# A deformable convolution: high and low parts of a tap's transposed values by one instruction each over two PSUM banks, not one per bank

## The chip, the cores and the metric

The kernel runs on one NeuronCore of a Trainium2 chip. The metric is the device time of one execution in microseconds (us), the lower the better. PE is the matrix engine (TensorE), PEld its weight loads, ACT the scalar engine, DVE the vector engine, POOL the engine that issues the gathers, SP the one that issues most loads and stores.

## The reference, cut to what matters

The input `x` is 4 images of 1024 channels and 64x64 pixels. Layer 0 is a bottleneck with a deformable 3x3 convolution, layer 1 a masked, grouped bottleneck. The change lies in the deformable convolution:

```python
out = jax.nn.relu(frozen_bn(conv2d(x, w1, stride=1), g1, b1, m1, v1))        # 1024 -> 256 channels
offset = conv2d(out, w_off, pad=1, bias=b_off)                               # 18 offsets for each pixel
# deform_conv3x3: for each of the 9 taps four gathered corners, weighted and summed
val = gather(y0, x0) * (wy0 * wx0)[:, None] + gather(y0, x1) * (wy0 * wx1)[:, None] + ...
out = jnp.einsum('nckhw,ock->nohw', val, w.reshape(w.shape[0], w.shape[1], K))
out = jax.nn.relu(frozen_bn(out, g2, b2, m2, v2))
out = frozen_bn(conv2d(out, w3), g3, b3, m3, v3)                             # 256 -> 1024 channels
return jax.nn.relu(out + x)
```

Layer 1 multiplies by a mask, convolves in 4 groups (1x1, 3x3, 1x1), adds its input and clips at zero.

## The kernel before, in words

The work is cut into 32 blocks of 8 image rows (512 pixels). A software pipeline of 42 steps runs five stages on different blocks at once. Stage A (first convolution) works on block s, stage T (offsets) on s-1, stage B (deformable convolution) on s-8, stage C (third convolution and the first of layer 1) on s-9, and stage E (the rest of layer 1) on s-10. So stage B runs in steps 8 to 39, and steps 8 to 31 have stage A beside it. Each engine has its own queue with an order written by hand, and the engines meet by semaphores. Steps are written in pairs; the middle of the program is a loop over such pairs, and "even" and "odd" steps below are the two halves of a pair.

Stage B of one block goes through 9 taps. For each tap, POOL gathers four tiles of 128 pixels (each with its four corners) into 8 slots, so two taps' gathers are in flight. ACT multiplies the first corner (`corner0`, L698), DVE adds the other three (`interpolate`, L952, 12 instructions), and the sum lies in `val` with pixels in the partitions. PE turns it (`turn_val`, L482): 8 transposes of 128x128 into two PSUM banks `psV[0]` and `psV[1]`, one for each half m of the 256 channels. The product is made in split precision: ACT copies each bank, rounded, to `valT_hi` (`valT_copy`, L712), DVE subtracts that copy from the bank to get `valT_lo` (`valT_low`, L962). Then PE multiplies (`tap`, L501 to L503: 12 matmuls, three products for each m and each output half o).

`psV`, `valT_hi` and `valT_lo` exist once. So these waits tie the engines together:

- `turn_val(k)` needs `val` of tap k, and that DVE has read `psV` for tap k-1 (`valT_rest`).
- `valT_copy(k)` needs the turned values and that the matmuls of tap k-1 are through (`tap_done`).
- `valT_low(k)` needs `valT_copy(k)` (`valT_ready`).
- `tap(k)` needs both parts.

PE's order in one step is, for k from 0 to 8: the work of other stages that is listed beside tap k, then `turn_val(k)`, then `tap(k-1)`. While ACT and DVE split tap k, PE has the work that stands beside tap k+1:

```python
                    1: each(conv3, 2, 3),
                    2: [lambda: conv1(1, 0), lambda: conv1(1, 1)],
...
                    8: each(gconv3, 0) + [lambda: conv1(0, 0, ahead=1, chunks=[0])],
```

DVE's order puts `valT_low(k-1)` first in its list for tap k. The exceptions are tap 8, whose low part is made in the same step behind a part of the interpolation, and whatever stage work stands ahead of it. ACT's order for a tap is work of other stages, `valT_copy(k)`, `corner0(k+2)`; for tap 1 the work ahead of it is four `y_relu` (L731). The gather of tap k+2 is released when DVE has finished the interpolation of tap k.

## Time and profile before

| | |
|---|---|
| median of 3 runs | 3049.81 us (3049.41 to 3057.76) |
| the profiled execution | 3054.81 us, of it 3053.0 us between first and last instruction |
| PE busy | 2839.3 us, 93% |
| DVE busy | 2311.4 us, 76% |
| ACT busy | 1290.1 us, 42% |
| POOL busy | 1233.8 us, 40% |
| mean granted PE clock | 0.979 of full speed |

Busy times overlap, so they don't add up to the span. A row of the timeline gives the start, how long a run of like instructions took, the engine, the source line, the operation, output and inputs, and how many instructions were merged. A bracket at its end gives how long the engine had been idle before and what ended that idle time. A row with x2 whose time is 1.08 us is two instructions that overlap in part, not two of 0.54 us.

### The profile page before, as it was taken

The numbers are of one execution on the slowest core, as the hardware profiler recorded it, in microseconds if no ns is written. First come the engines' busy times: TensorE is split into PE (matmuls) and PEld (weight loads), VectorE is DVE, ScalarE is ACT, GpSimd is POOL, SyncE is SP. The second block draws the span as 40 slices with busy tenths as digits, with TensorE's granted clock in tenths as the row PEclk, the third lists the DMA queues.
The fourth block names the chain that finished last, engine by engine and source line by source line (L and its number), as shares of the span: only waits on it lengthen the run. The fifth ranks groups of instructions, "written<-read, shape, count | busy, mean of one in ns | idle before, by whom it ended". The sixth has DMA issues, their size and how long they took to land.

```text
span 3053.0 us, 45120 instructions
## 1 busy us (share of the span) xinstructions
PE 2839.3 (93%) x12064; PEld 1564.4 (51%) x12064; DVE 2311.4 (76%) x5439; ACT 1290.1 (42%) x2530; POOL 1233.8 (40%) x1160
## 2 busy tenths in 40 slices
PE   7978999999999999999999999999999999999998
PEld 3435555555555555555555545555555555555553
DVE  2238888887788878788877778888778888888871
ACT  1224444444444444444444444444444444444442
POOL 1035444433434443344443434444434455555540
PEclk9989999999999999999999999999999999999999
DMA  7768887888788888888788788888887788888872
GB/s 265 233 225 318 316 288 274 310 299 296 277 298 270 314 291 298 286 295 290 273 306 298 274 290 277 291 307 300 289 287 275 278 303 290 296 295 299 294 269 83
DMA packets 263070, 863.50 MB, mean 283 GB/s; under 512 B 31746, under 2 KB 72834, under 8 KB 254336
## 3 DMA queue, kind: packets, MB, share of 16 engines
q0 software_dynamic: 165888, 604.05, 57.1%
q1 hardware_dynamic: 78592, 190.68, 17.9%
q10 hardware_dynamic: 18432, 67.12, 5.4%
q8 instruction: 44, 0.72, 0.1%
q14 instruction: 114, 0.93, 0.1%
HBM read 747.72 MB, written 114.02 MB: 282 GB/s over the span
## 4 chain that ended last, share of the span: by engine, by line
PE 63%; DMA 13%; DVE 10%; issue 7%; POOL 3%; ACT 2%; DVEq 0%; SPq 0%; ACTq 0%; POOLq 0%
DMA corners<-corner_tables,samples_in 13%; PE psR L521 9%; PE psA L413 8%; PE psD L501 7%; PE psD L503 7%; PE psD L502 7%; PE psR L553 6%; PE psV L482 6%; DVE val L952 6%; PE psA L449 4%; PE psR L534 4%; PE psR L570 3%; POOL corners L378 3%; PE psD L449 1%; DVE y L935 1%
## 5 line engine op out<-in xcount | busy, mean ns | idle before, releaser
L378 POOL DMA_INDIRECT corners<-corner_tables,samples_in x1152 | 1221.7, 1061 | 1722.7 <-DVE val L952 1268.8
L952 DVE SCALAR_TENSOR_TENSOR val<-corners,samples_in,val 128x256 f32<-128x256 f32 x3456 | 1426.8, 477 | 220.0 <-ACT val L698 179.8
L698 ACT ACTIVATE val<-corners,samples_in 128x256 f32<-128x256 f32 x1152 | 517.5, 505 | 371.1 <-DMA corners<-corner_tables,samples_in 365.9
L712 ACT ACTIVATE valT_hi<-psV 128x512 fp32r<-128x512 f32 x576 | 311.7, 593 | 802.1 <-PE psD L503 655.0
L521 PE MATMUL psR<-deformed,w_sb 128*128 128x512 f32 x1024 | 490.3, 620 | 60.3 <-DVE y L883 51.0
L962 DVE TENSOR_TENSOR valT_lo<-psV,valT_hi 128x512 fp32r<-128x512 f32 x576 | 370.0, 684 | 217.1 <-ACT valT_hi L712 216.6
L501 PE MATMUL psD<-valT_hi,w_hi 128*128 128x512 f32 x1152 | 488.8, 424 | 0.4 <-DVE valT_lo L962 0.4
L502 PE MATMUL psD<-valT_hi,w_lo 128*128 128x512 f32 x1152 | 460.1, 399 | 0.0
L503 PE MATMUL psD<-valT_lo,w_hi 128*128 128x512 f32 x1152 | 460.1, 399 | 0.0
L482 PEld LDWEIGHTS psV<-const_sb,val 128*128 128x128 f32 x2304 | 266.3, 143 | 240.9 <-issue 134.2
L482 PE MATMUL psV<-const_sb,val 128*128 128x128 f32 x2304 | 313.5, 279 | 72.9 <-DVE valT_lo L962 65.9
L413 PE MATMUL psA<-x_sb,w_sb 128*128 128x512 f32 x768 | 357.2, 604 | 6.2 <-DMA x_sb<-in_x 6.0
L521 PEld LDWEIGHTS psR<-deformed,w_sb 128*128 128x128 f32 x1024 | 195.2, 198 | 292.9 <-issue 197.1
L731 ACT ACTIVATE y<-y,bn_shift 128x512 f32<-128x512 f32 x256 | 179.7, 720 | 253.1 <-DVE y L883 253.0
L553 PE MATMUL psR<-ga,gw_sb 64*64 64x512 f32 x2304 | 261.5, 594 | 2.7 <-DVE ga L912 1.9
L501 PEld LDWEIGHTS psD<-valT_hi,w_hi 128*128 128x128 f32 x1152 | 220.9, 192 | 60.7 <-issue 17.8
L503 PEld LDWEIGHTS psD<-valT_lo,w_hi 128*128 128x128 f32 x1152 | 219.3, 190 | 54.0
L502 PEld LDWEIGHTS psD<-valT_hi,w_lo 128*128 128x128 f32 x1152 | 221.0, 192 | 42.3 <-issue 1.9
L413 PEld LDWEIGHTS psA<-x_sb,w_sb 128*128 128x128 f32 x768 | 140.7, 190 | 190.0 <-issue 177.6
L883 DVE SCALAR_TENSOR_TENSOR y<-psR,bn_scale,y 128x512 f32<-128x512 f32 x256 | 189.4, 742 | 28.5 <-PE psR L521 28.5
L570 PE MATMUL psR<-gb,gw_sb 64*128 64x512 f32 x512 | 144.5, 641 | 31.7 <-DVE gb L927 14.4
L553 PEld LDWEIGHTS psR<-ga,gw_sb 64*64 64x64 f32 x2304 | 83.0, 132 | 150.2 <-issue 150.2
(78 smaller groups left out, 1566.3 us busy)
## 6 DMA issues: line engine op xcount, KB each, us to landing
y<-in_x SPq DMA_DIRECT2D x128, 512.0 KB, 7.4
out<-y ACTq DMA_DIRECT2D x128, 512.0 KB, 7.7
x_sb<-in_x SPq DMA_DIRECT2D x48, 1024.0 KB, 8.3
corner_tables<-x_sb SPq DMA_DIRECT2D x128, 256.0 KB, 5.4
corners<-corner_tables,samples_in POOLq DMA_INDIRECT x1152, 6.0
y<-in_x SPq DMA_DIRECT2D x8, 2048.0 KB, 10.2
corner_tables<-corners SPq DMA_DIRECT2D x8, 1139.0 KB, 5.7
samples_dram<-samples SPq DMA_DIRECT2D x32, 90.0 KB
```

What stands on the lines that cost most here:

```text
L378: nc.gpsimd.indirect_dma_start(corners[:, slot, :], None, table, bass.IndirectOffsetOnAxis(ap=index[:, TAPS * t + k:TAPS * t + k + 1], axi ...
L413: mm = pe.matmul(psA[m][:], w1_sb[:, half * KC // 2 + k, m * P:(m + 1) * P], y[:, bpar, half * KC // 2 + k, :] if blow < LAG_B else x_sb[: ...
L482: mm = pe.transpose(psV[m][:, tile * P:(tile + 1) * P], val[:, (par + k) % 2, tile, m * P:(m + 1) * P], ident)
L501: pe.matmul(psD[o][:], w2_hi[:, m, k, chunk], valT_hi[:, m, :], start=first, stop=False)
L502: pe.matmul(psD[o][:], w2_lo[:, m, k, chunk], valT_hi[:, m, :], start=False, stop=False)
L503: mm = pe.matmul(psD[o][:], w2_hi[:, m, k, chunk], valT_lo[:, m, :], start=False, stop=last)
L521: mm = pe.matmul(psR[m % 2][:], w3_sb[:, k, m * P:(m + 1) * P], deformed[:, k, :], start=k == 0, stop=k == MC - 1)
L553: mm = pe.matmul(psR[half][64 * slot:64 * slot + 64, :], gw2_sb[rows, slot, j, :], ga[rows, par, slot, ky:ky + ROWS, kx:kx + IMG], start=j ...
L698: nc.scalar.activation(val[:, (bpar + k) % 2, tile, :], corners[:, n % GS, 0:CMID], ACT.Copy, scale=samples_in[:, bpar, w:w + 1]).then_inc ...
L712: nc.scalar.activation(valT_hi[:, m, :], psV[m][:], ACT.Copy).then_inc(valT_ready, 1)
L952: nc.vector.scalar_tensor_tensor(acc, corners[:, n % GS, corner * CMID:(corner + 1) * CMID], samples_in[:, bpar, w:w + 1], acc, ALU.mult, ...
L962: nc.vector.tensor_tensor(valT_lo[:, m, :], psV[m][:], valT_hi[:, m, :].bitcast(F32), ALU.subtract).then_inc(valT_rest, 1)
```

## The change

The two banks of `psV` become one PSUM tensor of 1024 values for each partition, `psV_both`; the names `psV[0]` and `psV[1]` are kept as its halves. ACT's two copies become one of 1024 values and DVE's two subtractions one of 1024. The semaphores `val_turned`, `valT_ready` and `valT_rest` count once for each tap, where they counted twice. The transposes go tile by tile with m inside, where they went m by m. `turn_val` waits once for `valT_rest` before its first transpose, where it waited before each half. `tap` waits once, before its first matmul, and for `valT_rest` alone.

```diff
-        psV = [ctx.enter_context(nc.psum_tensor(f"psV{i}", [P, 512], F32)) for i in range(2)]
+        psV_both = ctx.enter_context(nc.psum_tensor("psV", [P, MC * PIX], F32))
+        psV = [psV_both[:, i * PIX:(i + 1) * PIX] for i in range(MC)]
...
-                    for m in range(MC):
-                        if low > LAG_B or k >= 1:
-                            pe.wait_ge(valT_rest, 2 * (TAPS * h + k - 1) + m + 1)
-                        for tile in range(TILES):
+                    if low > LAG_B or k >= 1:
+                        pe.wait_ge(valT_rest, TAPS * h + k)
+                    for tile in range(TILES):
+                        for m in range(MC):
                             mm = pe.transpose(psV[m][:, tile * P:(tile + 1) * P],
                                               val[:, (par + k) % 2, tile, m * P:(m + 1) * P], ident)
-                        mm.then_inc(val_turned, 1)
+                    mm.then_inc(val_turned, 1)
...
                     for m in range(MC):
-                        pe.wait_ge(valT_ready, 2 * (TAPS * h + k) + m + 1)
-                        pe.wait_ge(valT_rest, 2 * (TAPS * h + k) + m + 1)
+                        if m == 0:
+                            pe.wait_ge(valT_rest, TAPS * h + k + 1)
...
-                        act.wait_ge(val_turned, 2 * (TAPS * block + k - 1))
+                        act.wait_ge(val_turned, TAPS * block + k - 1)
...
-                    for m in range(MC):
-                        act.wait_ge(val_turned, 2 * (TAPS * h + k) + m + 1)
-                        nc.scalar.activation(valT_hi[:, m, :], psV[m][:], ACT.Copy
-                                             ).then_inc(valT_ready, 1)
+                    act.wait_ge(val_turned, TAPS * h + k + 1)
+                    nc.scalar.activation(valT_hi[:].rearrange("p m x -> p (m x)"), psV_both[:], ACT.Copy
+                                         ).then_inc(valT_ready, 1)
...
-                    for m in range(MC):
-                        dve.wait_ge(valT_ready, 2 * (TAPS * h + k) + m + 1)
-                        nc.vector.tensor_tensor(valT_lo[:, m, :], psV[m][:],
-                                                valT_hi[:, m, :].bitcast(F32), ALU.subtract
-                                                ).then_inc(valT_rest, 1)
+                    dve.wait_ge(valT_ready, TAPS * h + k + 1)
+                    by_pair = lambda a: a.rearrange("p m x -> p (m x)")
+                    nc.vector.tensor_tensor(by_pair(valT_lo[:]), psV_both[:], by_pair(valT_hi[:]).bitcast(F32),
+                                            ALU.subtract).then_inc(valT_rest, 1)
```

On PE, in the loop over the middle steps, the turn of tap 2 stands behind the 8 matmuls of the first convolution (L413, in the changed kernel L414) that cover the split of tap 1. Before:

```order
L413 MATMUL psA<-x_sb,w_sb 128x512 [waits x_in]
L413 MATMUL psA<-x_sb,w_sb 128x512 x3
L474 REGISTER_ALU
L480 ISA [waits fma]
L482 MATMUL psV<-const_sb,val 128x128 [waits valT_rest]
L482 MATMUL psV<-const_sb,val 128x128 x3
L480 REGISTER_ALU
L482 MATMUL psV<-const_sb,val 128x128 [waits valT_rest]
L482 MATMUL psV<-const_sb,val 128x128 x3
L501 MATMUL psD<-valT_hi,w_hi 128x512 [waits valT_rest,valT_ready]
```

and in the changed kernel:

```order
L414 MATMUL psA<-x_sb,w_sb 128x512 [waits x_in]
L414 MATMUL psA<-x_sb,w_sb 128x512 x3
L475 REGISTER_ALU
L480 REGISTER_ALU [waits fma]
L483 MATMUL psV<-const_sb,val 128x128 [waits valT_rest]
L483 MATMUL psV<-const_sb,val 128x128 x7
L502 MATMUL psD<-valT_hi,w_hi 128x512 [waits valT_rest]
```

The order of the work is the same. The second wait, between the fourth and the fifth transpose, is gone, and the first one now stands for the whole low part of the tap before.

On ACT, at the same place of the program, the split of tap 1 stands behind the four `y_relu` (L731) and ahead of the first corners of tap 3 (L698, in the changed kernel L699). Before:

```order
L731 ACTIVATE y<-y,bn_shift 128x512 [waits y_sum] x4
L707 ISA
L711 REGISTER_ALU [waits tap_done]
L712 ACTIVATE valT_hi<-psV 128x512 [waits val_turned]
L711 REGISTER_ALU
L712 ACTIVATE valT_hi<-psV 128x512 [waits val_turned]
L693 ISA
L696 REGISTER_ALU [waits val_turned]
L698 ACTIVATE val<-corners,samples_in 128x256 [waits gathered0]
```

and in the changed kernel:

```order
L731 ACTIVATE y<-y,bn_shift 128x512 [waits y_sum] x4
L708 ISA
L711 REGISTER_ALU [waits tap_done]
L712 ACTIVATE valT_hi<-psV 128x1024 [waits val_turned]
L697 REGISTER_ALU [waits val_turned]
L699 ACTIVATE val<-corners,samples_in 128x256 [waits gathered0]
```

Nothing moved past anything else; two copies became one, and a register instruction or two went with them. DVE's order changes in the same way, two L962 of 128x512 to one of 128x1024.

## Rows read from the trace of the kernel before

**Rows 1.** The page: the span, and the chain that ended last, by engine.

```profile
span 3053.0 us, 45120 instructions
...
PE 63%; DMA 13%; DVE 10%; issue 7%; POOL 3%; ACT 2%; DVEq 0%; SPq 0%; ACTq 0%; POOLq 0%
```

**Rows 2.** The page's costliest groups: count, busy us, mean ns, idle before them.

```profile
L698 ACT ACTIVATE val<-corners,samples_in 128x256 f32<-128x256 f32 x1152 | 517.5, 505 | 371.1 <-DMA corners<-corner_tables,samples_in 365.9
L712 ACT ACTIVATE valT_hi<-psV 128x512 fp32r<-128x512 f32 x576 | 311.7, 593 | 802.1 <-PE psD L503 655.0
...
L962 DVE TENSOR_TENSOR valT_lo<-psV,valT_hi 128x512 fp32r<-128x512 f32 x576 | 370.0, 684 | 217.1 <-ACT valT_hi L712 216.6
...
L731 ACT ACTIVATE y<-y,bn_shift 128x512 f32<-128x512 f32 x256 | 179.7, 720 | 253.1 <-DVE y L883 253.0
```

**Rows 3.** Groups of instructions by shape, whole run: a DVE subtraction of 1024 columns.

```profile
L1011 DVE TENSOR_TENSOR w_lo<-x_sb,w_hi 128x1024 fp32r<-128x1024 f32 x1 | 1.2, 1217 | 0.0
```

**Rows 4.** Timeline of all engines about the turn of tap 8, step 21.

```profile
1421.60 1.08 ACT L712 ACTIVATE valT_hi<-psV 128x512 fp32r<-128x512 f32 x2 [5.08 <-PE psD L503]
1422.23 1.29 DVE L962 TENSOR_TENSOR valT_lo<-psV,valT_hi 128x512 fp32r<-128x512 f32 x2 [0.52 <-ACT valT_hi L712]
...
1422.48 1.13 PE L413 MATMUL psA<-x_sb,w_sb 128*128 128x512 f32 x2
1422.57 1.70 ACT L698 ACTIVATE val<-corners,samples_in 128x256 f32<-128x256 f32 x4
...
1423.44 1.28 DVE L935 TENSOR_TENSOR y<-psR,y 128x512 f32<-128x512 f32 x2
1423.44 1.04 PE L482 MATMUL psV<-const_sb,val 128*128 128x128 f32 x8
```

**Rows 5.** The chain that ended last, about the turn of tap 2, step 21.

```profile
1372.37 0.59 ACT valT_hi L712
...
1372.98 0.70 DVE valT_lo L962
...
1373.72 1.25 PE psV L482 x8
1374.97 0.24 PE psD L501
```

**Rows 6.** Timeline of all engines about the turn of tap 1, step 23.

```profile
1541.62 1.28 DVE L962 TENSOR_TENSOR valT_lo<-psV,valT_hi 128x512 fp32r<-128x512 f32 x2
...
1542.36 0.93 PE L482 MATMUL psV<-const_sb,val 128*128 128x128 f32 x5 [0.20 <-DVE valT_lo L962]
```

**Rows 7.** PE's timeline: the turn of tap 2, and the next transposes, in five steps.

```profile
1011.98 1.25 PE L482 MATMUL psV<-const_sb,val 128*128 128x128 f32 x8 [2.36 <-DVE valT_lo L962]
...
1015.88 1.04 PE L432 MATMUL psA<-const_sb,mid 128*128 128x128 f32 x8
...
1193.61 1.25 PE L482 MATMUL psV<-const_sb,val 128*128 128x128 f32 x8 [3.29 <-DVE valT_lo L962]
...
1556.83 1.71 PE L482 MATMUL psV<-const_sb,val 128*128 128x128 f32 x8 [2.73 <-DVE valT_lo L962]
...
2193.40 1.94 PE L482 MATMUL psV<-const_sb,val 128*128 128x128 f32 x8 [3.45 <-DVE valT_lo L962]
...
2199.71 1.03 PE L432 MATMUL psA<-const_sb,mid 128*128 128x128 f32 x8
...
2285.34 1.94 PE L482 MATMUL psV<-const_sb,val 128*128 128x128 f32 x8 [3.93 <-DVE valT_lo L962]
```

**Rows 8.** Windows: busy us by engine, then PE's granted clock, DMA share, GB/s.

```profile
1012.00:1018.00 6.00, 6.00 (x31) 4.54 (x32) 6.00 (x15) 4.46 (x11) 2.60 (x3) 1.00 0.86 293
...
2193.40:2199.40 6.00, 6.00 (x19) 5.09 (x20) 5.25 (x13) 2.54 (x6) 2.60 (x3) 0.53 0.84 285
```

**Rows 9.** Windows about the start of an odd step, columns as in rows 8.

```profile
1525.00:1530.00 5.00, 4.68 (x18) 1.92 (x16) 3.82 (x10) 3.02 (x7) 0.00 (x0) 1.00 0.26 107
...
1540.00:1545.00 5.00, 4.62 (x19) 2.86 (x20) 3.69 (x9) 0.51 (x1) 3.07 (x3) 1.00 1.04 432
```

**Rows 10.** Timeline of all engines about a turn in step 35, without stage A.

```profile
2649.49 1.28 DVE L962 TENSOR_TENSOR valT_lo<-psV,valT_hi 128x512 fp32r<-128x512 f32 x2
...
2650.69 1.27 DVE L952 SCALAR_TENSOR_TENSOR val<-corners,samples_in,val 128x256 f32<-128x256 f32 x3
...
2650.93 0.82 PE L482 MATMUL psV<-const_sb,val 128*128 128x128 f32 x6
```

## The prediction, made before the changed kernel had run

> **What bounds the kernel now.** I read the page first. PE has 63% of the chain that ended last, the gathers' DMA 13% and DVE 10% [rows 1]. So time is lost or won where PE waits, and at the start of a step, where the gathers end last. The groups come next [rows 2]: DVE stood idle 216.6 us before the low part of a tap, each time released by ACT's high part, while ACT itself was idle 655.0 us waiting for PE's last matmul. Neither engine is short of time there. What counts is latency: from the moment PE frees `valT_hi` until PE may overwrite `psV`. The third view is the timeline about each turn of a tap, to see how much other work covers that latency.
>
> At the turn of tap 8 the cover is thin [rows 4]. ACT starts at 1421.60, DVE at 1422.23, and PE, busy until then with two half-matmuls of the first convolution, turns at 1423.44 without any idle time. At the turn of tap 2 in odd steps there is no cover left [rows 5]: the chain runs ACT, DVE, PE. ACT's copies stand late there, behind four `y_relu` that wait for the values gathered at the step's start.
>
> **The duration of the new pair.** A DVE subtraction of 1024 columns took 1.217 us from SBUF [rows 3]; I take it for PSUM too: it is 0.53 us more than the 0.684 of the low part's 512 columns [rows 2], about a column a nanosecond. No row has an ACT copy of 1024 columns. From below: ACT took 505 ns for 256 columns and 593 for 512 [rows 2], other operand kinds, and by that slope 1024 take 0.77 us. From above: two copies took 1.08 us end to end [rows 4]. Between them, 505 ns for 256 columns and 720 for 512 with a bias [rows 2] give 0.84 ns a column, hence 0.593 + 0.430 = 1.02 us, which I take because both rows have per-partition operands and the slope is the steeper, surer one.
>
> What the engines save is small. The pair holds ACT 0.97 us (1421.60 to 1422.57) and DVE 1.21 us (1422.23 to 1423.44) [rows 4]. One instruction of 1.02 or 1.217 us, overlapping its successor by some 0.08 as these do, holds them 0.94 and 1.14. That is 0.03 and 0.07 us for each of 288 taps, 29 us of engine time in all, costed at nothing: at most taps both wait for PE's matmuls, and that idle time swallows it. If this cover were gone it would be worth those 29 us.
>
> **What the pair's latency does.** Before, DVE began 0.61 us after ACT (1372.37 to 1372.98), PE began to turn 0.74 after that, at 1373.72, needing only the first half, and was through at 1374.97 [rows 5], 2.60 us after ACT's start. The turn took 1.25 and not the usual 1.04 [rows 4], because its second half waited for DVE too. Now the steps are ACT 1.02, hand-over 0.04, DVE 1.217, hand-over 0.06: PE may start 2.34 us after ACT and is through 1.04 later, at 3.38. So a turn that waits loses 3.38 - 2.60 = 0.78 us. Where DVE comes late of its own and ACT has long finished, before was 0.74 + 1.25 = 1.99 after DVE's start [rows 5, 6], now 1.217 + 0.06 + 1.04 = 2.32: a loss of 0.33.
>
> I went through all 288 taps with this arithmetic, taking for each the starts of ACT, DVE and PE from the timeline. Four terms remain.
>
> 1. *Turn of tap 8, steps 8 to 31.* ACT starts at 1421.60, so PE may start at 1423.94, and it was ready at 1423.44: 0.50 us lost [rows 4]. All 24 steps show a loss, 0.32 to 0.75; together **12.0 us**. Nothing behind it absorbs the shift: the last taps, the output adds, the last interpolation and the next gathers all follow PE.
> 2. *Turn of tap 2, odd steps from 11 to 29 and steps 12, 30 and 31*: 13 places, with a wait for `valT_rest` of 1.94 to 3.93 us (five shown) [rows 7]. Nine run at full clock and lose 0.78 each, 7.0 us. Four run at the low clock, where the second half didn't wait separately, and lose the whole later start, 2.34 - 1.35 = 0.99 each, 4.0 us. Together **11.0 us**.
> 3. *The clock.* In the same places PE's wait grows. The row at 1011.98, after 2.36 us of idle time, and the one at 1193.61, after 3.29, ran at clock 1.00, which is 2.4 GHz. Those at 2193.40 and 2285.34, after 3.45 and 3.93, ran near 0.53, the level of 1.2 GHz for most of the window, and the one at 1556.83 after 2.73 did too in part, with another short wait just before [rows 7, 8]. From turn to the next transposes 3.90 us passed at full clock (1011.98 to 1015.88) and 6.31 at the low one (2193.40 to 2199.71) [rows 7]. The 3.90 holds 0.21 us of waiting for the second half, so a fall costs 2.6 us, and 1.6 where it is partial (two of the four such places). I take 2.1. The wait grows by 0.99, less 0.33 because the turn of tap 1 and with it the first convolution start later [rows 6], so by 0.66. Nine waits of 1.94 to 3.29 become 2.6 to 3.95; six of them become longer than the 3.45 of the row at 2193.40. Six at 2.1 are **12.6 us**, with 0 and nine at 2.6, 23 us, as the ends.
> 4. *Steps 8 to 10*, where PE still waits at other taps: about **2 us**, an estimate by the same two prices.
>
> The turn of tap 1 in odd steps starts late by 0.33 [rows 6], but the turn of tap 2 then waits for DVE anyway, so this costs nothing. In even steps it has room. In the last eight steps, without stage A, DVE frees `psV` 1.28 us after its start, at 2650.77, where PE turned at 2650.93 [rows 10]: 0.16 us of cover, so nothing is lost. The matmuls' single wait costs nothing at taps 0 to 7, as the next turn has already waited for the same event; at tap 8 six more matmuls stand between, which cover it.
>
> The sum is 12.0 + 11.0 + 12.6 + 2 = 37.6 us. On the profiled execution that is 3054.8 + 37.6 = 3092. That execution lies 5 us above the median of 3049.81, so against the median I expect 3087.
>
> A rule of the skill speaks against this change. The Trainium skill, Perfetto Trace Analysis, section Optimizing Scalar/DVE Operations, says that where Scalar and Vector aren't saturated but cause bubbles on other engines, breaking up instructions may let work complete sooner. The change does the reverse, and the rows agree with the rule: ACT and DVE idle, PE waits.
>
> The same section advises grouping into larger operations if the engine is saturated; by that the 29 us of engine time would be a gain, which is the rival on the other side below.
>
> **The rivals.**
>
> - *Waits alone, no new falls of the clock.* Terms 1, 2 and 4: 25 us, 3075. For it: the row at 1193.61 kept the full clock after 3.29 us of idle time. Against it: the one at 1556.83 did not after 2.73 [rows 7]. The Trainium skill, TensorE: Matmul & The Clock Gate, section HAM oscillation, tells of waits between groups of matmuls that throw the clock to half; by that page more of the nine would fall.
> - *All nine fall, and ACT's copy takes 1.08.* Term 3 is 23 us, terms 1 and 2 grow by 0.06 x 37 = 2: 50 us, 3100. Each further 0.1 us of the pair, should two banks cost extra, adds 0.1 x 37 = 3.7 us.
> - *Hidden anyway.* The 12 odd steps start with gathers at a DMA share of 1.04, so a later PE might cost nothing there. But at 1525 to 1530, when the shift arrives, the share is 0.26 [rows 9], so the queue isn't backlogged. If hidden, half of term 1 goes. With ACT at 0.77 the waits shrink by 0.25 x 37 = 9 more. Both and no clock fall: 25 - 6 - 9 = 10 us, 3060, the edge of no change.
> - *Faster: engine time counts after all.* If ACT's and DVE's own occupancy set the pace, 29 us are gained, 3021. It decides only where neither waits for PE between two taps; the idle sums of [rows 2] are against it.
>
> **How the numbers follow.** Forecast with four to nine falls 0.48, waits alone 0.26, above that 0.06, hidden to within 0.3% (9 us, about what a measurement of this kernel can tell from no change) 0.14, faster 0.06. The range 3062 to 3102 takes in the first two and part of the third. Slower 0.80, same 0.14, faster 0.06.
>
> **What the profile after would show.** ACT's L712 at about 1.02 us and DVE's L962 at 1.217. DVE's idle time before the low part up by about 0.4 us at each tap where it waited. PE's idle time before the transposes, for `valT_lo`, up by some 20 us, with waits of about 0.5 at tap 8, where there were none. The turn of tap 2 in odd steps after waits above 3 us, more of them at the low clock. Wrong would be: transposes of tap 8 without a wait (then ACT's copy is much shorter than 1.02), or a step's start that absorbs the shift.

## The result: slower by 2.0%, more than was predicted

| | median | lowest to highest | runs |
|---|---|---|---|
| before, beside it | 3053.78 us | 3049.41 to 3058.21 | 4 |
| changed | 3116.68 us | 3108.91 to 3118.46 | 4 |

The ratio is 1.0203, with an interval from 1.0181 to 1.0225: 63 us more. Predicted were 3087 us and a range up to 3102, so the sign was right and the size too small. The profiled execution of the changed kernel took 3108.91 us, at the lower end of its runs, and its mean granted clock was 0.971 against 0.979.

The page of the changed kernel, with the rows that answer to [rows 1, 2] and the gathers' group. A group's row has count, busy us, mean ns, then the idle time before it. The gathers' group of the kernel before stands first, as it was not among the rows shown:

```profile
L378 POOL DMA_INDIRECT corners<-corner_tables,samples_in x1152 | 1221.7, 1061 | 1722.7 <-DVE val L952 1268.8
```

and the changed kernel:

```profile
span 3107.1 us, 43186 instructions
...
PE 62%; DVE 12%; DMA 10%; issue 9%; ACT 3%; POOL 2%; DVEq 1%; SPq 0%; ACTq 0%; POOLq 0%
...
L379 POOL DMA_INDIRECT corners<-corner_tables,samples_in x1152 | 1246.1, 1082 | 1750.2 <-DVE val L952 1297.2
...
L712 ACT ACTIVATE valT_hi<-psV 128x1024 fp32r<-128x1024 f32 x288 | 293.7, 1020 | 838.2 <-PE psD L504 649.6
L962 DVE TENSOR_TENSOR valT_lo<-psV,valT_hi 128x1024 fp32r<-128x1024 f32 x288 | 352.1, 1223 | 304.0 <-ACT valT_hi L712 264.5
```

The two durations are those that were worked out: 1.020 us for ACT and 1.223 for DVE. So there is no surprise in the instructions themselves. DVE's idle time behind ACT grew from 216.6 to 264.5 us. One row moved that the prediction never looked at: the gathers on POOL take 1246.1 us for the same 1152 instructions, 24 us more than their 1221.7 before. The sum alone doesn't tell the time, though: after_pad16 below has 1246.9 us there too and is 34 us faster.

**The turn of tap 8 (answers to [rows 4]).** Timeline of the changed kernel, step 21.

```profile
1440.33 1.02 ACT L712 ACTIVATE valT_hi<-psV 128x1024 fp32r<-128x1024 f32 x1 [4.77 <-PE psD L504]
...
1441.20 1.12 PE L414 MATMUL psA<-x_sb,w_sb 128*128 128x512 f32 x2
...
1441.38 1.23 DVE L962 TENSOR_TENSOR valT_lo<-psV,valT_hi 128x1024 fp32r<-128x1024 f32 x1 [0.58 <-issue]
...
1442.66 1.09 PE L483 MATMUL psV<-const_sb,val 128*128 128x128 f32 x8 [0.34 <-DVE valT_lo L962]
```

PE turns 2.33 us after ACT's start, where 2.34 was worked out. The turn now stands behind 0.34 us of idle time. From L414's start to the turn pass 1.46 us, before it was 0.96 from L413's start: the 0.50 us of term 1. Over the whole trace PE's idle time before the transposes grew from 72.9 to 93.8 us, the "some 20 us" that was forecast.

**The turn of tap 2 (answers to [rows 7, 8]).** PE's timeline of the changed kernel in three of the thirteen steps, from the turn to the next transposes.

```profile
840.97 1.09 PE L483 MATMUL psV<-const_sb,val 128*128 128x128 f32 x8 [2.86 <-DVE valT_lo L962]
844.70 1.04 PE L433 MATMUL psA<-const_sb,mid 128*128 128x128 f32 x8
...
1206.60 1.10 PE L483 MATMUL psV<-const_sb,val 128*128 128x128 f32 x8 [3.19 <-DVE valT_lo L962]
1211.88 0.38 PE L433 MATMUL psA<-const_sb,mid 128*128 128x128 f32 x2
...
1574.81 1.09 PE L483 MATMUL psV<-const_sb,val 128*128 128x128 f32 x8 [2.12 <-issue]
```

The windows of the first two, where the third figure from the right is PE's granted clock:

```profile
840.97:844.70 3.73, 3.73 (x21) 3.14 (x21) 3.73 (x10) 1.61 (x3) 1.15 (x1) 1.00 0.93 293
...
1206.60:1211.88 5.28, 5.28 (x20) 4.29 (x21) 4.69 (x12) 1.61 (x3) 2.11 (x2) 0.68 0.77 287
```

The piece takes 3.73 us at the full clock and 5.28 where the clock had fallen after 3.19 us of idle time: a fall costs 1.55 us. In step 19 it is new; before, 3.29 us of idle time there left the clock at 1.00 [rows 7]. In step 23 the wait even became shorter, 2.12 after 2.73 us. The row of step 19 ends with the view's window, so its x2 is not the whole group.

The turn of tap 1 in step 23, which answers to [rows 6]:

```profile
1560.65 1.21 DVE L962 TENSOR_TENSOR valT_lo<-psV,valT_hi 128x1024 fp32r<-128x1024 f32 x1
...
1561.92 1.09 PE L483 MATMUL psV<-const_sb,val 128*128 128x128 f32 x8 [0.73 <-DVE valT_lo L962]
```

PE turns 1.27 us after DVE's start, where it had turned after 0.74, and takes 1.09 us instead of 1.25 (in [rows 6] 0.93 of it are shown, as the row is cut at the window's edge): through at 2.36, worked out 2.32.

**The steps without stage A (answers to [rows 10]).** Here lies what the prediction missed. First PE's timeline in step 35 of the kernel before, behind the turn of tap 6 at 2642.55. L570 is a grouped convolution of stage E, L576 adds the input by a matmul, and behind them comes the turn of tap 7 at 2650.93 [rows 10].

```profile
2648.05 1.13 PE L570 MATMUL psR<-gb,gw_sb 64*128 64x512 f32 x4 [1.60 <-DVE gb L927]
2649.10 1.98 PE L576 MATMUL psR<-y,const_sb 128*128 128x512 f32 x4
```

The same place of the changed kernel, from turn to turn:

```profile
2674.11 1.09 PE L483 MATMUL psV<-const_sb,val 128*128 128x128 f32 x8
...
2681.60 1.21 PE L571 MATMUL psR<-gb,gw_sb 64*128 64x512 f32 x4 [3.59 <-DVE gb L927]
2682.74 3.55 PE L577 MATMUL psR<-y,const_sb 128*128 128x512 f32 x4
2686.13 1.04 PE L483 MATMUL psV<-const_sb,val 128*128 128x128 f32 x8
```

and the windows of its two halves:

```profile
2677.80:2681.60 3.80, 0.21 (x1) 0.00 (x1) 3.32 (x8) 2.13 (x4) 0.69 (x1) 1.00 0.99 362
2682.74:2686.13 3.39, 3.39 (x7) 1.40 (x5) 3.39 (x7) 1.50 (x3) 2.76 (x3) 0.53 0.50 118
```

From turn to turn 8.38 us became 12.02. PE waits 3.59 us for DVE's `gb` instead of 1.60, and behind the longer wait it runs at clock 0.53, near the level of 1.2 GHz, so that four matmuls take 3.55 us instead of 1.98. Why `gb` is late is seen on POOL and DVE, some 10 us earlier. The kernel before:

```profile
2633.49 1.19 POOL L378 DMA_INDIRECT corners<-corner_tables,samples_in  x1 [5.64 <-DVE val L952]
...
2633.78 1.28 DVE L962 TENSOR_TENSOR valT_lo<-psV,valT_hi 128x512 fp32r<-128x512 f32 x2
...
2634.98 0.94 POOL L378 DMA_INDIRECT corners<-corner_tables,samples_in  x1 [0.30 <-issue]
...
2634.98 4.84 DVE L952 SCALAR_TENSOR_TENSOR val<-corners,samples_in,val 128x256 f32<-128x256 f32 x12
...
2636.22 1.24 POOL L378 DMA_INDIRECT corners<-corner_tables,samples_in  x1 [0.30 <-issue]
...
2637.77 2.87 POOL L378 DMA_INDIRECT corners<-corner_tables,samples_in  x1 [0.30 <-issue]
```

and the changed kernel:

```profile
2665.05 1.19 POOL L379 DMA_INDIRECT corners<-corner_tables,samples_in  x1 [5.63 <-DVE val L952]
...
2665.35 1.22 DVE L962 TENSOR_TENSOR valT_lo<-psV,valT_hi 128x1024 fp32r<-128x1024 f32 x1
...
2666.48 4.83 DVE L952 SCALAR_TENSOR_TENSOR val<-corners,samples_in,val 128x256 f32<-128x256 f32 x12
...
2666.55 1.22 POOL L379 DMA_INDIRECT corners<-corner_tables,samples_in  x1 [0.30 <-issue]
...
2668.08 4.05 POOL L379 DMA_INDIRECT corners<-corner_tables,samples_in  x1 [0.30 <-issue]
...
2672.43 0.94 POOL L379 DMA_INDIRECT corners<-corner_tables,samples_in  x1 [0.30 <-issue]
...
2675.96 0.49 DVE L952 SCALAR_TENSOR_TENSOR val<-corners,samples_in,val 128x256 f32<-128x256 f32 x1 [2.18 <-ACT val L699]
2678.28 2.07 DVE L952 SCALAR_TENSOR_TENSOR val<-corners,samples_in,val 128x256 f32<-128x256 f32 x5 [1.83 <-ACT val L699]
2680.26 1.28 DVE L927 SCALAR_TENSOR_TENSOR gb<-psR,maskx 128x512 f32<-128x512 f32 x2
```

Read POOL against DVE. In both kernels the gathers of a tap, but for the first, fall beside or just behind twelve interpolations that DVE runs with nothing between them (called a stretch below). One gather is much longer than the others, and is called held here. It ends 0.82 us after the last of the twelve: before, 2637.77 + 2.87 = 2640.64 and 2634.98 + 4.84 = 2639.82; changed, 2668.08 + 4.05 = 2672.13 and 2666.48 + 4.83 = 2671.31. What differs is which gather it is. Before, it is the fourth, that begins 2.79 us into the stretch. In the changed kernel DVE passes from the low part to the stretch sooner (2665.35 to 2666.48 are 1.13 us, where 2633.78 to 2634.98 are 1.20), so the stretch begins before the second gather instead of with it. That gather takes 1.22 us instead of 0.94, and the third is caught 1.60 us into the stretch and held for 4.05. The fourth then can begin only at 2672.43, 1.12 us after the stretch's end; before, it had ended 0.82 us after that point. Its corners come late, the first corner on ACT too, DVE waits 2.18 and 1.83 us (before 0.38 and 2.02) ahead of `gb`, and PE waits for `gb`.

In most of the steps from 32 on, two taps' gathers meet such a stretch. There are 14 held gathers of 4.04 to 4.06 us instead of 13 of 2.86 to 2.87. Fourteen times 1.18 us are 16.5 us.

### The profile page after: what moved, and what is told of

Same layout as the page of the kernel before. It is cut to its first block, busy times and chain, and to the rows that moved or that the text cites. A ratio compares the mean times of both kernels' runs of the same rounds, so it can differ in the third digit from the quotient of the medians.

```text
span 3107.1 us, 43186 instructions
## 1 busy us (share of the span) xinstructions
PE 2856.0 (92%) x12064; PEld 1570.8 (51%) x12064; DVE 2290.9 (74%) x5151; ACT 1274.7 (41%) x2242; POOL 1258.1 (40%) x1160
## 4 chain that ended last, share of the span: by engine, by line
PE 62%; DVE 12%; DMA 10%; issue 9%; ACT 3%; POOL 2%; DVEq 1%; SPq 0%; ACTq 0%; POOLq 0%
DMA corners<-corner_tables,samples_in 10%; PE psR L522 9%; PE psA L414 7%; PE psD L502 7%; PE psD L503 7%; PE psD L504 7%; DVE val L952 6%; PE psV L483 6%; PE psR L554 6%; PE psA L450 4%; PE psR L535 4%; PE psR L571 2%; DVE valT_lo L962 2%; POOL corners L379 2%; PE psR L577 1%
## 5 line engine op out<-in xcount | busy, mean ns | idle before, releaser
L379 POOL DMA_INDIRECT corners<-corner_tables,samples_in x1152 | 1246.1, 1082 | 1750.2 <-DVE val L952 1297.2
L699 ACT ACTIVATE val<-corners,samples_in 128x256 f32<-128x256 f32 x1152 | 515.8, 500 | 370.1 <-DMA corners<-corner_tables,samples_in 352.8
L712 ACT ACTIVATE valT_hi<-psV 128x1024 fp32r<-128x1024 f32 x288 | 293.7, 1020 | 838.2 <-PE psD L504 649.6
L962 DVE TENSOR_TENSOR valT_lo<-psV,valT_hi 128x1024 fp32r<-128x1024 f32 x288 | 352.1, 1223 | 304.0 <-ACT valT_hi L712 264.5
L483 PE MATMUL psV<-const_sb,val 128*128 128x128 f32 x2304 | 311.0, 279 | 93.8 <-DVE valT_lo L962 76.5
L414 PE MATMUL psA<-x_sb,w_sb 128*128 128x512 f32 x768 | 356.5, 603 | 5.2 <-DMA x_sb<-in_x 5.2
L731 ACT ACTIVATE y<-y,bn_shift 128x512 f32<-128x512 f32 x256 | 179.3, 718 | 272.2 <-DVE y L883 247.7
L414 PEld LDWEIGHTS psA<-x_sb,w_sb 128*128 128x128 f32 x768 | 141.2, 190 | 187.2 <-issue 177.3
```

The source lines that it names most:

```text
L379: nc.gpsimd.indirect_dma_start(corners[:, slot, :], None, table, bass.IndirectOffsetOnAxis(ap=index[:, TAPS * t + k:TAPS * t + k + 1], axi ...
L414: mm = pe.matmul(psA[m][:], w1_sb[:, half * KC // 2 + k, m * P:(m + 1) * P], y[:, bpar, half * KC // 2 + k, :] if blow < LAG_B else x_sb[: ...
L483: mm = pe.transpose(psV[m][:, tile * P:(tile + 1) * P], val[:, (par + k) % 2, tile, m * P:(m + 1) * P], ident)
L699: nc.scalar.activation(val[:, (bpar + k) % 2, tile, :], corners[:, n % GS, 0:CMID], ACT.Copy, scale=samples_in[:, bpar, w:w + 1]).then_inc ...
L712: nc.scalar.activation(valT_hi[:].rearrange("p m x -> p (m x)"), psV_both[:], ACT.Copy).then_inc(valT_ready, 1)
L962: nc.vector.tensor_tensor(by_pair(valT_lo[:]), psV_both[:], by_pair(valT_hi[:]).bitcast(F32), ALU.subtract).then_inc(valT_rest, 1)
```

## Where the time went

The stretches between PE's turns, added up in each trace, give the table. Single executions differ by several us in parts whose code is the same. The changed kernel, after_pad16, after_pad384 and after_break have the changed code in the steps with stage A; the kernel before, without_a, before_pad384 and before_break have the old code there. So the rows for steps 8 to 31 compare the means of four traces with four.

| part | predicted | measured | from |
|---|---|---|---|
| turn of tap 7 to turn of tap 8, steps 11 to 31 | 10.5 of 12.0 | 10.8 | 133.3 - 122.5 |
| the rest of steps 11 to 31 (terms 2 and 3) | 23.6 | 10.7 | 1924.2 - 1902.7, less 10.8 |
| steps 8 to 10 | 2, and 1.5 of term 1 | 8.0 | 251.75 - 243.75 |
| steps 32 to 39 | 0 | 35.8 | 647.3 - 611.5, this kernel's trace |

The sum is 65 us, and the medians differ by 63. The first row is firm: its four traces lie at 132.2 to 134.1 us, the four of before at 122.4 to 122.7. The second is less so, since the four traces of before differ by 12 us among themselves over steps 11 to 31. By place, those 10.7 us are 3.8 between the turns of taps 0 and 1, 2.4 between 1 and 2, 4.2 between 2 and 3, and 0.4 behind the turn of tap 8. In the last row 30.1 us lie between the turns of taps 6 and 7 of the seven steps 33 to 39. Of these, 16.4 are PE's idle time before the first matmul on `gb` (26.6 us in all instead of 10.2), and 13.7 are what passes from there to the turn (35.2 instead of 21.4, each rounded): all seven ran at the low clock, before only one had.

## The experiments

All are built on the kernel before or on the changed one. Each median stands beside the kernel before on the same chip: 3051.51 us for the first four, 3056.83 for the next four, 3054.81 for the last four. The ratio is not exactly the quotient of the two medians; it differs from it by up to 0.0016.

| kernel | what it has | median us | ratio (interval) |
|---|---|---|---|
| with_a | one instruction each in steps with stage A | 3095.22 | 1.0135 (1.0106 to 1.0164) |
| without_a | one instruction each in the other steps | 3081.41 | 1.0107 (1.0076 to 1.0138) |
| dve_one | two high parts, one low part | 3131.00 | 1.0256 (1.0226 to 1.0285) |
| act_one | one high part, two low parts | 3073.08 | 1.0066 (1.0040 to 1.0092) |
| after_pad16 | changed, 0.07 us of DVE work behind a low part | 3082.51 | 1.0088 (1.0066 to 1.0110) |
| after_pad384 | changed, 0.38 us of it | 3071.00 | 1.0062 (1.0041 to 1.0083) |
| before_pad384 | before, 0.38 us of it | 3048.13 | 0.9974 (0.9960 to 0.9989) |
| after_break | changed, DVE's long stretches broken up | 3080.73 | 1.0076 (1.0054 to 1.0099) |
| split_7 | with_a, tap 7 with two instructions | 3074.49 | 1.0061 (1.0043 to 1.0079) |
| split_1 | with_a, tap 1 with two instructions | 3073.82 | 1.0063 (1.0045 to 1.0081) |
| split_017 | with_a, taps 0, 1 and 7 with two | 3057.63 | 1.0007 (0.9992 to 1.0023) |
| before_break | before, DVE's long stretches broken up | 3045.49 | 0.9967 (0.9954 to 0.9981) |

### Which steps, and which engine

The kernel keeps both forms and chooses by the step (`on` lists the stages of a step) or by the engine. `tap` keeps its two pairs of waits everywhere in these kernels and in the split ones below, where the changed kernel has one wait.

```diff
+        psV_both = ctx.enter_context(nc.psum_tensor("psV", [P, MC * PIX], F32))
+        one_copy = lambda on: "A" in on       # without_a: "A" not in on; act_one: True; dve_one: False
+        one_low = lambda on: "A" in on        # without_a: "A" not in on; act_one: False; dve_one: True
+        one_turn = lambda on: "A" in on       # without_a: "A" not in on; act_one, dve_one: False
...
+                    if one_copy(on):
+                        act.wait_ge(val_turned, 2 * (TAPS * h + k) + 2)
+                        nc.scalar.activation(by_pair(valT_hi[:]), psV_both[:], ACT.Copy).then_inc(valT_ready, 2)
+                        return
```

Steps with stage A alone:

> One instruction for each part in the steps that have stage A beside B (8 to 31), two as before in steps 32 to 39. Theory 1 (two places, two causes: PE waits longer at the turns of taps 8 and 2 in the middle steps, and something separate in the last eight): about half of the loss, +20 to +28 us over the kernel before (3054), so 3074 to 3082, and the turn of tap 7 in steps 33 to 39 as before. Rival (one cause, a state of the transfers that the middle steps hand on to the last ones): the whole +62.

Steps without stage A alone:

> The reverse: one instruction for each part in steps 32 to 39 alone. Theory 1: +28 to +34 us, so 3082 to 3088, all of it between the turns of taps 6 and 8 and at the step's end in steps 33 to 39, with gathers on POOL that take 4.05 us where 2.86 stood. Rival: no loss, since the middle steps are those of before.

The steps with stage A cost 44 us, where 20 to 28 were expected, and those without it 30, as expected. The second number is the clear one: where the prediction had put nothing lies nearly half of the loss. The trace of without_a has 30.1 us between the turns of taps 6 and 7, as the changed kernel has, and the same 14 gathers held for 4.04 to 4.06 us. Together the two are 74 us, 11 more than the whole change. The three intervals together leave some 15 us either way, so this doesn't show that the two halves interact. The trace of with_a, its fastest execution of five, shows some 37 of its 44 (34 in steps 8 to 31, against the mean of four, and 2.5 behind them). A part of that is the experiment's own: its turn of tap 8 waits 0.46 us in most steps, where the changed kernel has 0.34, which over the 21 steps from 11 on is 2.6 us.

Two high parts and one low part:

> Two high parts as before, one low part of 1024 columns, in all steps. Theory 1 with the gathers' hold set by where DVE's low part ends (0.07 us sooner with one instruction): the tail's +31 us remains, the middle is about the same as in the changed kernel, since the low part starts after 1.08 us of copies, not 1.02: about +60, 3114. Rival (the longer copy on ACT is what hurts): most of the loss gone, below +20.

One high part and two low parts:

> One high part of 1024 columns, two low parts and the two waits of the turn as before. Theory 1: the tail as before, with holds of 2.86 us. In the middle PE may start a turn 0.45 us later than before where DVE waits for ACT: 0.45 x 13 = 6 us at tap 2, 0.17 x 24 = 4 at tap 8, so +10, 3064. Rival (ACT's copy hurts): +40 or more.

The groups of the high and low part, first in dve_one, then in act_one:

```profile
L730 ACT ACTIVATE valT_hi<-psV 128x512 fp32r<-128x512 f32 x576 | 311.6, 592 | 832.5 <-PE psD L517 680.4
L980 DVE TENSOR_TENSOR valT_lo<-psV,valT_hi 128x1024 fp32r<-128x1024 f32 x288 | 352.0, 1222 | 327.8 <-ACT valT_hi L730 327.5
```

```profile
L726 ACT ACTIVATE valT_hi<-psV 128x1024 fp32r<-128x1024 f32 x288 | 294.1, 1021 | 833.6 <-PE psD L517 656.6
L985 DVE TENSOR_TENSOR valT_lo<-psV,valT_hi 128x512 fp32r<-128x512 f32 x576 | 370.2, 684 | 269.4 <-ACT valT_hi L726 268.8
```

The one low part is the costly half of the change. It costs 80 us alone, where 60 were expected, and more than the change itself. It must wait for two copies that take longer than one (1.08 against 1.02 us), and DVE's idle time behind ACT is 327.5 us. But 0.06 us at the 37 places where PE waits are an estimate of 2 us, so most of the excess over the change is not explained. The one high part alone costs 22, which makes 3073 where 3064 was expected. As dve_one keeps the old order of the transposes and both waits of the turn and of `tap`, and loses more, neither the new order nor the single waits are needed for the loss; they weren't run alone. The tail tells the two apart as well: dve_one has 14 gathers of 4.05 us and 31.8 us more between the turns of taps 6 and 7, act_one has 13 of 2.87 us and 1.9 more. So the long holds come with DVE's single subtraction, whatever ACT does.

### Is it the moment at which the gathers meet DVE's stretch?

If 0.07 us less between gather and stretch cause the hold, giving DVE 0.07 us back should undo it. In the steps without stage A a write to an unused tile stands behind the low part of taps 0 to 7; it takes 0.07 us with 16 columns and 0.38 with 384. Nothing of the computation changes.

```diff
+        pad_sb = sb("pad_sb", [P, 16])        # pad384: [P, 384]
...
+                    nc.vector.memset(pad_sb[:], 0.0).then_inc(padded, 1)
...
+                if "A" not in on:
+                    for k in range(1, TAPS):
+                        beside[k].insert(1, lambda k=k: pad(k))
```

> The changed kernel with one small write more on DVE (16 columns, to a tile nobody reads) behind each low part in steps 32 to 39 but for tap 8's, so that the interpolation there starts later by some 0.05 to 0.1 us, about where two low parts would have let it start. Theory 2 (the tail's loss is gathers on POOL that are held until a stretch of twelve interpolations ends, and which gather is held is decided by where its start falls in that stretch): the holds go back from 4.05 to 2.86 us or vanish, and the time falls by 25 to 32 us from 3117 although DVE has more to do. Rival (the low part's own later end costs the tail its time, by latency): the same 3117 or up to 3 us more.

> The same with 384 columns, which moves the stretch by some 0.3 to 0.5 us. Theory 2: the gathers start at other places of the stretch, near those of the middle steps, which were not held (their fourth gather began 2.38 us into the stretch, the held ones 2.78): no holds of 2.86 or 4.05 in the tail, time 25 to 50 us below 3117. Rival: 8 steps x 8 x 0.4 us more work on DVE, +0 to +15 over 3117.

> The kernel before (two instructions for each part) with the same write of 384 columns behind each low part in steps 32 to 39. Theory 2: the 13 holds of 2.86 us in the tail vanish or change; without them each saves about 1.9 us of a gather, so 3054 falls by up to 20 us. Rival: equal or slower by up to 10 us.

POOL and DVE in step 35 of after_pad16:

```profile
2662.10 0.07 DVE L976 MEMSET pad_sb<- 128x16 f32 x1
...
2662.13 0.94 POOL L382 DMA_INDIRECT corners<-corner_tables,samples_in  x1 [0.30 <-issue]
...
2663.38 1.22 POOL L382 DMA_INDIRECT corners<-corner_tables,samples_in  x1 [0.31 <-issue]
...
2664.90 2.86 POOL L382 DMA_INDIRECT corners<-corner_tables,samples_in  x1 [0.30 <-issue]
```

The pattern of the kernel before is back: 0.94, 1.22, and 2.86 us for the fourth gather. A program with 64 writes more is 34 us faster than the changed kernel (3116.68 to 3082.51; each has its own runs of the kernel before beside it, and the two ratios are 1.0203 and 1.0088). The stretch between the turns of taps 6 and 7 falls to 5.4 us above the kernel before, where it had been 30.1.

With 384 columns no gather of the tail is held at all, in either kernel: the fourth begins 2.27 us into the stretch there, takes 0.94, and both traces have 6 us less than the kernel before between the turns of taps 6 and 7. The write's own time is paid at the turn of tap 2 (1 to 2: about 10 us), but before_pad384 is still faster than the kernel before by 0.26%.

### Or is it the stretch itself?

Moving the gathers' moment and breaking DVE's stretch are two ways to the same end. Here the same 16-column write stands between the first and second four of the twelve interpolations, and between the second and third four, at the two places of a step where all twelve run without a break.

```diff
+                if "A" not in on:
+                    for n, (k, i) in enumerate([(5, 3), (5, 2), (7, 3), (7, 2)]):
+                        beside[k].insert(i, lambda n={(5, 2): 0, (5, 3): 1, (7, 2): 2, (7, 3): 3}[k, i]: pad(n + 1))
```

> The changed kernel with the small write of 16 columns between the three corners of two interpolations in steps 32 to 39 (those made in the lists of taps 5 and 7), so that the start of the stretch stays where it was and the stretch is broken in three. Theory 2 with the hold lasting until DVE's row of like instructions is interrupted: a hold ends at the first break behind its start, at most 1.7 us, and the time falls by 20 to 30 us from 3117. If such a break doesn't free POOL, the holds last 4.1 to 4.2 us and the time stays at 3117.

> The kernel before, with the small write of 16 columns between the three corners of two interpolations in steps 32 to 39 (four for each step). Theory of the held gathers: the holds of 2.86 us in the tail go, as in the changed kernel with the same breaks, and the time falls by 5 to 12 us below the kernel before (3046 for 3055), as with the write of 384 columns. Rival (it was the later start alone that helped): 3055.

POOL and DVE in step 35 of after_break, where the gathers begin as in the changed kernel:

```profile
2664.87 2.07 DVE L955 SCALAR_TENSOR_TENSOR val<-corners,samples_in,val 128x256 f32<-128x256 f32 x5
2664.93 1.22 POOL L382 DMA_INDIRECT corners<-corner_tables,samples_in  x1 [0.30 <-issue]
2666.46 0.94 POOL L382 DMA_INDIRECT corners<-corner_tables,samples_in  x1 [0.30 <-issue]
2666.49 0.07 DVE L976 MEMSET pad_sb<- 128x16 f32 x1
2667.70 1.23 POOL L382 DMA_INDIRECT corners<-corner_tables,samples_in  x1 [0.30 <-issue]
```

and in step 35 of before_break:

```profile
2628.76 0.07 DVE L977 MEMSET pad_sb<- 128x16 f32 x1
2629.93 0.94 POOL L381 DMA_INDIRECT corners<-corner_tables,samples_in  x1 [0.30 <-issue]
...
2639.26 1.13 PE L573 MATMUL psR<-gb,gw_sb 64*128 64x512 f32 x4 [0.65 <-DVE gb L930]
```

In after_break the third gather, which began 1.60 us into the stretch and took 4.05 us in the changed kernel, begins 1.59 us behind the stretch's start (2664.87 to 2666.46) and takes 0.94. The view merges the fifth interpolation, which starts beside the write, with the four before it, hence x5. No gather of the tail is held in either kernel, and in before_break PE's idle time before the matmul on `gb` is 0.65 us in step 35, where 1.60 was. The changed kernel comes down to 3080.73 us. The kernel before becomes faster than it was by 0.33% (0.19 to 0.46), 3045.49 against 3054.81: 32 writes that compute nothing save 9 us. It beats both kernels and has the lowest ratio of all, though before_pad384's interval overlaps with its.

### What is left in the steps with stage A

With the tail as before, with_a is split again at single taps. Splitting tap 7 gives PE back its early turn of tap 8, splitting tap 1 that of tap 2. The code below is cut to the choice of the taps.

```diff
+        SPLIT = (7,)                          # split_1: (1,); split_017: (0, 1, 7)
+        one = lambda on, k: "A" in on and k % TAPS not in SPLIT
```

> One instruction for each part in the steps with stage A but for tap 7, which is split by two instructions each, as everything in steps 32 to 39. Compared with the run of one instruction in all taps of those steps (3095, its turns of tap 8 13.4 us late in sum). Theory: the turn of tap 8 waits no longer, 12 to 14 us less, 3082. Rival (the loss there is taken back by a wait further on, since the next step's start waits for the gathers anyway): 3093 or more.

> The same with tap 1 alone split in two. Theory: the turn of tap 2 in odd steps starts 0.99 us and ends 0.78 us sooner, 11 us, and up to 13 more if fewer of these places run at the low clock: 3071 to 3086. Rival (what the turn of tap 2 loses is nothing, as the profiled run showed 0.9 us there): 3093 or more.

> Taps 0, 1 and 7 split in two, the others by one instruction, in the steps with stage A. Theory: every turn that had no cover is as before, and the six merged taps have cover, so the time is that of the kernel before, 3054 to 3062, with some 14 us less busy time on DVE and ACT that nobody needs. Rival (merged taps cost or give something by themselves): more than 10 us away from it.

By medians with_a is 43.7 us above the kernel before, split_7 19.7, split_1 19.0, and split_017 2.8, which can't be told from nothing. So all of the loss in these steps lies at taps 0, 1 and 7, and the six other taps may have their single instructions at no cost that can be measured: PE has other work there, as the prediction said. Splitting tap 7 and splitting tap 1 give 24 and 25 us, each with some 10 us of doubt either way by the intervals. For split_7 that is more than the 12 to 14 us expected, but not clear of them, and the 49 us together are more than the 41 that all three taps give. Tap 0 wasn't split alone. The traces show the two waits that were meant. In split_7 the turn of tap 8 has no idle time before it in steps 10 to 30, where with_a has 0.46 to 0.74 us. In split_1 the thirteen waits before the turn of tap 2 sum to 31.2 us, where with_a has 43.8 and the kernel before 38.9. (The profiled execution of split_7, 3089.3 us, is the longest of its six, so its sums are not used.)

## Why the prediction was wrong

In short: the steps with stage A were forecast to lose 37.6 us and lost about 30, and the last eight steps were forecast to lose nothing and lost 36. The sign was right for a reason, since the first part of the loss is there and is where it was said to be. That the two errors point different ways, and so leave the total at 63 and not at 73 or more, is luck.

**Right.** Both durations, to 0.01 us (1.020 for 1.02, 1.223 for 1.217). PE may turn 2.33 us after ACT's start for the 2.34 worked out. Term 1: 0.50 us at the turn of tap 8 in each middle step, 10.8 us of the 10.5 that it had there. The taps with other work beside them cost nothing, as split_017 shows.

**Mis-sized: terms 2 and 3, the turn of tap 2 and the clock, 23.6 us for a measured 10.7.** Term 3 had nine places at the full clock before, and six new falls at 2.1 us. The trace of before has seven of the thirteen at the low clock already, not four; one that was counted as full is step 13:

```profile
647.81 1.25 PE L482 MATMUL psV<-const_sb,val 128*128 128x128 f32 x8 [3.23 <-DVE valT_lo L962]
...
653.26 1.03 PE L432 MATMUL psA<-const_sb,mid 128*128 128x128 f32 x8
```

From turn to transposes 5.45 us passed there, against 3.90 at the full clock, the same 1.55 that a fall costs in the changed kernel. In the means of four traces 5.5 places become 9.75, and 4.25 falls at 1.55 are 6.6 us where 12.6 stood, which leaves some 4 us for term 2, where 11.0 stood. The thirteen waits grew from 36.4 to 42.1 us, 0.45 us each and not the 0.66 of term 3; and from the turn to the next transposes 0.17 us less pass at the full clock (3.73 for 3.90), which takes 2.2 us back. Against that, 3.8 us were lost between the turns of taps 0 and 1, where the prediction had put nothing. The four and four traces leave each of these sums some us of doubt. The rival "waits alone" came nearer in size, with 11.0 for both, though its ground was wrong: the clock did fall more often. The step that failed is "nine run at full clock", and with it "six of them become longer than the 3.45": a bound on the length of the wait told neither where the clock fell before nor where it fell afterwards.

**Mis-sized: steps 8 to 10**, 8.0 us where 2 and their part of term 1 (1.5) stood. The trace of the changed kernel has, over the three steps together, 1.0 to 1.3 us more in each of the stretches between the turns of taps 0, 1, 2 and 3, 2.8 more from tap 5 to tap 6, and 1.6 behind tap 8. This was not taken apart further.

**The step that failed, and made the forecast too small: "In the last eight steps, without stage A [...] 0.16 us of cover, so nothing is lost."** The 0.16 us was right for PE and `psV`, and it was the wrong question. Nothing is lost at the turn; the loss came by way of POOL. That engine stands in none of the prediction's sums. The chain is: DVE's pair is 0.07 us shorter; the third gather begins 1.60 us into a stretch of twelve interpolations instead of 1.24; it is held for 4.05 us; the corners behind it are late; `gb` is late by 2 us; PE's wait passes 3 us and the clock falls to 0.53. The experiments show the first links, and that the loss between these turns hangs on them; the links from the corners to PE's clock are read from the traces. after_pad16 breaks the chain at its first link, after_break at its second, and each takes the 30 us away: between those turns 5.4 us more than the kernel before are left in the one, 4.1 less than it in the other.

**Failed with it: the engine time "costed at nothing".** The 0.07 us for each tap were looked at as a gain that might be hidden or not, 29 us at most. They were a loss: a shorter instruction moved the gathers to a worse moment against DVE. The rival "faster" looked at the right quantity with the wrong sign; that its 29 us are near the 30 that were lost there is chance, since the loss isn't made of these 0.07 us.

The rule in the Trainium skill, Perfetto Trace Analysis, section Optimizing Scalar/DVE Operations, that breaking up instructions may help where Scalar and Vector aren't saturated but cause bubbles elsewhere, is borne out in the middle steps: splitting tap 1 and tap 7 again is worth 24 to 25 us each by the medians, with the doubt given above.

**What stays open.** Where a gather is held is known in part, and the cause is not known. Counted over all fourteen traces, for stretches of twelve with no other row between: of the gathers that began 1.58 to 1.60 us into one, 49 of 57 were held; at 2.77 to 2.79, 103 of 105; at 2.38 to 2.40, all in the steps with stage A, 25 of 110; about 1.24 and at 2.26 to 2.27, none. So the position goes with the hold but doesn't settle it. Some gathers are held for 1.7 to 3.3 us in steps 11 to 31, 5 of them before and 4 changed. One kind of these, a pair of 2.5 and 1.9 us behind the turn of tap 1, can be priced: in the even steps from 12 to 28 of the seven kernels that have it, the 30 steps with the pair took 92.9 us in the mean and the 33 without it 92.3. A kernel that has both the broken stretches and single instructions at taps 2 to 6 and 8 wasn't run; by split_017 and before_break I estimate that it would be no faster than before_break, since those single instructions gave nothing.

## What to carry to other kernels

Merging two instructions into one saves engine time and adds latency; look first for the waits that the first half used to release, and price only those places. Then ask what a few hundredths of a microsecond do to everything else that the engine works beside: here gathers issued by POOL were held by an unbroken run of vector instructions, and a shift of 0.07 us between the two cost 30 us. Where a POOL row with a steady duration shows an odd long one, lay it beside DVE's timeline, and try a tiny instruction of another kind in the middle of the run.

## What the runs showed of the hardware

**A gather instruction on POOL is held by an unbroken stretch on DVE.** In the last eight steps the held ones ended 0.82 us after the last of twelve SCALAR_TENSOR_TENSOR of 128x256 (4.83 us), after 2.87 or 4.05 us instead of 0.94 to 1.24. A MEMSET of 16 columns (0.07 us) between two of the twelve let them through. All ten kernels with the unbroken stretch at or near its usual place (after_pad16 among them) had 10 to 14 such holds in the last eight steps; the four with a shifted or broken one (after_pad384, before_pad384, after_break, before_break) had none.

The Trainium skill, SBUF — State Buffer, section Who interferes with whom, says that DVE and GpSimd share a pair of ports as an exclusive lock that a DVE instruction with two SBUF inputs can hold against a GpSimd instruction that reads SBUF, not against one that only writes it. The interpolation has such inputs, so the page may point to a cause, if a gather counts as a reader, which no run here shows. It speaks of one instruction at a time. Here the hold outlasts up to eight of them and ends with the whole stretch, and by the measurement that is what holds in this kernel; no run here shows that the port is the reason.

**The clock after idle time isn't told by the length of the last wait alone.** Before the turn of tap 2, 3.29 us left it at 1.00 in the kernel before and 3.19 us brought it down in the changed one, to 0.68 over the next 5.28 us. In the tail all seven places fell behind waits of 3.51 to 4.60 us, and of the seven before, with waits of 0.79 to 2.03 us, only the one behind 2.03 did.

**The second bank shows no cost of its own.** One instruction over both, 1.020 us on ACT and 1.223 on DVE, is the one-bank duration plus about 0.43 and 0.54 us for 512 columns more. For DVE that is the 1.217 us of 1024 columns from SBUF [rows 3] to 0.01 us.
